# Block 1 of a quantized weight placed in two halves, and the first condition weights issued from another queue

## The reference

```python
W = weights[condition]                      # weights 16 x 64 x 64, condition 64
y = jnp.einsum('bct,bcd->bdt', x, W)        # x 64 x 64 x 1024, float32
v0 = p[:, :, 0] & 63; v1 = p[:, :, 0] >> 6 & 63; v2 = p[:, :, 1] & 63; v3 = p[:, :, 2] & 63
w = (unpacked.astype(jnp.float32) - zero_point) * scale      # 1024 x 1024, from qweight 1024 x 768 int32
out = x + jnp.einsum('bsk,nk->bsn', y, w) + bias
```

## Time and profile before

| | |
|---|---|
| median of the runs | 285.45 us |
| profiled execution | 285.6 us |
| its span, first to last instruction | 283.8 us |
| TensorE busy | 277.3 us, 98% of the span |
| VectorE busy | 191.8 us, 68% |
| ScalarE busy | 83.8 us, 30% |
| GpSimd busy | 99.2 us, 35% |
| granted TensorE clock, mean | 0.998 |

### The profile page before, as it was taken

The page is one execution under the profiler, slowest core; times in us unless marked ns, Lnnn a source line. Parts: engine busy times, 40 slices in busy tenths (PEclk is TensorE's granted clock), DMA queues, the critical chain, the costliest instruction groups (busy, mean ns, idle before and its releaser), DMA issues.

```text
span 283.8 us, 8491 instructions
## 1 busy us (share of the span) xinstructions
PE 277.3 (98%) x3307; PEld 231.4 (82%) x3307; DVE 191.8 (68%) x261; ACT 83.8 (30%) x169; POOL 99.2 (35%) x41
## 2 busy tenths in 40 slices
PE   7999999899999999999999999999999999999995
PEld 3888888788888888988888888888888888888885
DVE  2898897785566566865559555676667655595554
ACT  3795334241044300633017310443106330060000
POOL 4005903964430444314442444404443044430000
PEclk9999999999999999999999999999999999999999
DMA  7930563446215541355114551145413562101112
GB/s 277 372 120 11 179 223 133 155 162 223 75 74 157 168 174 67 112 160 198 74 74 124 165 211 74 74 155 157 155 69 113 161 209 90 74 37 74 74 74 75
DMA packets 20278, 37.96 MB, mean 134 GB/s; under 512 B 6814, under 2 KB 7070, under 8 KB 20266
## 3 DMA queue, kind: packets, MB, share of 16 engines
q1 hardware_dynamic: 19322, 35.43, 36.6%
q10 hardware_dynamic: 944, 2.38, 2.3%
HBM read 21.02 MB, written 16.78 MB: 133 GB/s over the span
## 4 chain that ended last, share of the span: by engine, by line
PE 95%; DMA 2%; issue 1%; ACT 1%; DVE 0%; SPq 0%
PE o_ps L296 71%; PE y_ps L296 12%; PE y_ps L265 10%; DMA w_sb<-in_L_cond_weights_dram 2%; PE o_ps L265 1%; PE o_ps L278 0%; DMA ids<-in_itok_B_dram 0%; PE o_ps L307 0%; ACT qT L446 0%; PE y_ps L278 0%; PE y_ps L307 0%; ACT y_hi L430 0%; SPq L163 0%; DVE o_sb L625 0%; DVE o_sb L627 0%
## 5 line engine op out<-in xcount | busy, mean ns | idle before, releaser
L296 PE MATMUL o_ps<-qT,y_hi 128*128 128x512 f32 (+1 forms) x448 | 171.5, 386 | 0.5 <-ACT qT L446 0.5
L296 PE MATMUL o_ps<-qT,y_lo 128*128 128x512 f32 (+1 forms) x448 | 171.2, 385 | 0.0
L647 POOL TENSOR_TENSOR resid<-x_sb,bias_bc 128x1024 f32<-128x1024 f32 x32 | 95.8, 3001 | 151.1 <-DVE o_sb L549 130.7
L296 PEld LDWEIGHTS o_ps<-qT,y_hi 128*128 128x128 f32 x448 | 83.6, 188 | 17.5 <-ACT qT L446 0.7
L296 PEld LDWEIGHTS o_ps<-qT,y_lo 128*128 128x128 f32 x448 | 83.6, 188 | 16.8
L541 DVE TENSOR_TENSOR o_sb<-o_ps,scale_bc 128x512 f32<-128x512 f32 x54 | 37.4, 692 | 73.5 <-PE o_ps L296 73.5
L430 ACT ACTIVATE y_hi<-y_ps 128x512 fp32r<-128x512 f32 x56 | 29.4, 610 | 96.7 <-PE y_ps L265 96.4
L549 DVE TENSOR_TENSOR o_sb<-o_sb,resid 128x512 f32<-128x512 f32 x63 | 51.5, 822 | 1.9
L421 ACT ACTIVATE junk<-x_sb 128x1024 bf16<-128x1024 f32 x32 | 33.9, 1058 | 63.3 <-DMA x_sb<-in_x_dram 63.3
L530 DVE SCALAR_TENSOR_TENSOR resid<-zs_bc,ysum,resid 128x1024 f32<-128x1024 f32 x32 | 44.8, 1403 | 0.0
L520 DVE TENSOR_TENSOR y_lo<-y_ps,y_hi 128x512 fp32r<-128x512 f32 x57 | 35.7, 689 | 5.4 <-ACT y_hi L430 5.4
(11 more groups left out here) (44 smaller groups left out, 71.1 us busy)
## 6 DMA issues: line engine op xcount, KB each, us to landing
x_sb<-in_x_dram SPq DMA_DIRECT2D x32, 512.0 KB, 3.4
out_dram<-o_sb SPq DMA_DIRECT2D x63, 256.0 KB, 2.1
q_raw<-in_L_ffn_qweight_dram ACTq DMA_DIRECT2D x6, 384.0 KB, 5.8
w_sb<-in_L_cond_weights_dram SPq DMA_DIRECT2D x63, 16.0 KB, 2.0
q_raw<-in_L_ffn_qweight_dram SPq DMA_DIRECT2D x2, 384.0 KB, 7.4
out_dram<-o_sb SPq DMA_DIRECT2D x2, 128.0 KB, 1.9
ids<-in_itok_B_dram SPq DMA_DIRECT2D x1, 0.2 KB
w_sb<-in_L_cond_weights_dram ACTq DMA_DIRECT2D x1, 16.0 KB, 3.6
```

Of the source, the lines that this page charges most:

```text
L296: last = nc.tensor.matmul(bank, part[:, slot, kt, :], qT[:, kt, col:col + width], start=(kt == 0 and part is y_hi), stop=(kt == KT - 1 and ...
L647: nc.gpsimd.tensor_tensor(resid[:, j % RING, :], x_sb[:, j % RING, :], bias_bc[:], ALU.add).then_inc(xbias_ready, 1)
```

## The change

Tile 0's condition weights are both issued from ScalarE's queue, each after its number is read. SyncE reads the two numbers of tile 1, issues tile 1 of x, and then both halves of tile 1's condition weights. Block 1 is placed by two instructions of 512 elements a row instead of one of 1024, with a semaphore after each, and the products of `y_hi` in `first_quarter` wait for the first half before their first four and for the second before their last four. VectorE no longer waits for ScalarE before it copies half 1 of `y_hi`; the wait, now for both halves, stands before `y_lo`.

```diff
             load_x(0, 0)
             sp.wait_ge(ids_loaded, 16)
-            load_w_half(sp, 0, 0, pick_first(sp, 0))
+            picked = [pick_first(sp, 2 + half) for half in range(2)]
             load_x(1, 0)
             for half in range(2):
-                load_w_half(sp, 1, half, pick_first(sp, 2 + half))
+                load_w_half(sp, 1, half, picked[half])
...
+            pe.wait_ge(qt_ready, 1)
+            pe.wait_ge(qt_half_ready, 1)
+            pe.wait_ge(y_hi_ready, 2)
+            first_quarter(y_hi, range(0, KT // 2))
             pe.wait_ge(qt_ready, 2)
-            pe.wait_ge(y_hi_ready, 2)
-            first_quarter(y_hi)
+            first_quarter(y_hi, range(KT // 2, KT))
...
+            def place_q_halves(n):
+                act.wait_ge(qt_ps_ready, n + 1)
+                for half, done in enumerate((qt_half_ready, qt_ready)):
+                    kts = slice(half * (KT // 2), (half + 1) * (KT // 2))
+                    nc.scalar.activation(qT[:, kts, n * P:(n + 1) * P], qt_banks[n % 2].bitcast(I16)[:, kts, :],
+                                         ACT.Copy, bias=-QCENTER).then_inc(done, 1)
...
-            load_w_half(act, 0, 1, pick_first(act, 1))
+            for half in range(2):
+                load_w_half(act, 0, half, pick_first(act, half))
             for n in (2, 3, 5, 7):
                 load_q(act, n)
             place_q(0)
             high(0, 0, y_banks[0], range(1))
-            place_q(1)
+            place_q_halves(1)
...
+                if whole:
+                    dve.wait_ge(y_hi_ready, t * 2 + 2)
                 for half in range(2):
-                    dve.wait_ge(y_hi_ready, t * 2 + half + 1)
+                    if not whole:
+                        dve.wait_ge(y_hi_ready, t * 2 + half + 1)
...
             dve.wait_ge(y_ps_ready, 2)
-            dve.wait_ge(y_hi_ready, 1)
             nc.vector.tensor_copy(y_hi[:, 0, :, S:2 * S], y_banks[0][1]).then_inc(y_hi_ready, 1)
-            low(0, 0, y_banks[0])
+            low(0, 0, y_banks[0], whole=True)
```

More of the change, by code:

```diff
@@ L122, in adaln_ffn @@
         qt_ready = sem("qt_ready")
+        qt_half_ready = sem("qt_half_ready")
         warm_ready = sem("warm_ready")
@@ L355, in left_half, with first_quarter @@
                 return products(o_ps[:, 0, :], 0, NH, 1, kts)
-            def first_quarter(part):
-                return products(o_ps[:, 0, 0:2 * P], 0, 2 * P, 0, parts=(part,))
+            def first_quarter(part, kts=range(KT)):
+                return products(o_ps[:, 0, 0:2 * P], 0, 2 * P, 0, kts, parts=(part,))
             pe.wait_ge(warm_ready, 1)
@@ L513, in spread, with low @@
                 nc.vector.stream_shuffle(row[:], row[:], mask=[0] * QUADRANT).then_inc(s, 1)
-            def low(j, i, banks):
+            def low(j, i, banks, whole=False):
                 t = i * RING + j
+                if whole:
+                    dve.wait_ge(y_hi_ready, t * 2 + 2)
                 for half in range(2):
-                    dve.wait_ge(y_hi_ready, t * 2 + half + 1)
+                    if not whole:
+                        dve.wait_ge(y_hi_ready, t * 2 + half + 1)
                     cols = slice(half * S, (half + 1) * S)
```

## The result

The changed kernel takes 288.23 us (median of 6 runs, 287.43 to 289.52) against 285.53 us (6 runs, 285.0 to 285.9): ratio 1.0089, 95% interval 1.0068 to 1.0111, so slower by 0.9% or about 2.5 us (the medians differ by 2.7). Forecast were 286.15 us and a range of 285.0 to 286.6. The direction was right, the size was not. The execution profiled first is the shortest of the six, 287.43 us with a span of 285.6.

The account below looks back on a forecast made before the run. TensorE was taken to bound the kernel without slack. The work edits' -0.34 us, with q2 landing 1.05 us later, came to +0.71: profiled 285.6 becomes 286.3, or 286.15 us against the median, range 285.0 to 286.6.

Parts of the forecast that it names:

- The bound and the carry: TensorE, busy 277.3 of 283.8 us: any shift at the start of tile 0's `y_lo` products (10.89 us) passes fully into the time.
- VectorE's wait and the two halves: Start-up, block 1: copy without its wait and placing in halves start the `y_lo` products near 10.55, not 10.89: -0.34 us.
- The order of transfers: DMA queues at start-up: tile 1 of x goes ahead of q2 and of tile 0's second weight half, making q2 late.
- q2 lands 1.05 us later: q2's DMA behind tile 1 of x: landing at 8.65 instead of 7.6, `y_lo` products at 11.60, +0.71 us in all.
- bounds of 0.95 and 1.28: q2's delay in us: 0.95 if moved side by side with tile 1 of x, 1.28 if wholly behind it.
- transfers of 128 rows proceed nearly in the order of issue: Trace reading of the start-up DMAs: large transfers go one after another, not side by side, at 0.41 MB/us.
- The condition weights: Rival, chance 0.12: tile 0's second weight half lands behind all of tile 1, at 8.15; mix at 8.29; +0.95, 286.4 us.
- its sign of 1.4 us: TensorE waiting over 1.4 us for tile 0's condition weights would show that the weights case holds.
- Of these nothing is waited for at its old time: SyncE's queue: tile 1 of x, its weights, q4 and q6 go out earlier, q4 and q6 about a microsecond; no cost counted.
- The clock: TensorE after the longer waits: a granted clock below 1.00 would add a cost, counted at nothing.
- Instruction fetch: Rival, chance 0.07: shifted code makes TensorE's 1.2 us wait near 49 us vanish or grow, 284.9 or 287.3 us.

Follow-up runs that it names:

- e1_compute: The changed kernel with the DMA queues of the kernel before, so only the work edits remain; 285.75 us, ratio 0.9999 to the kernel before.
- e7_cold: The changed kernel without the two warm-up matmuls ahead of tile 0's mix; 288.75 us, ratio 1.0101 to the kernel before.
- e11_x1_first: The kernel before with one line moved: SyncE issues tile 1 of x right behind tile 0, before waiting for the condition numbers; 287.74 us, ratio 1.0058.
- e4_x1_last: The changed kernel with both halves of tile 1's condition weights issued ahead of tile 1 of x on SyncE's queue; 288.81 us, ratio 1.0091 to the kernel before.
- the second profile: Profile of a repeat of the changed kernel, unaltered; the repeat measured 289.20 us, ratio 1.0118 to the kernel before.
- e3_q46_last: The changed kernel with q4 and q6 issued behind the three rows on SyncE's queue, after q3, q5 and q7; 288.00 us, ratio 1.0087 to the kernel before.
- e14_q2_first: The changed kernel with only one of three rows ahead of tile 1 of x, its weights behind, q4 and q6 last; 287.08 us, ratio 1.0050 to the kernel before.

## Why the prediction was right or wrong

**The bound and the carry: right from the sums on, wrong before them.** The loop adds nothing to a shift. But "whatever the change does to the start of tile 0's `y_lo` products is what it does to the time" doesn't hold. These products came 1.12 us later and the sums 1.58, with the wait for q3 between them. For a gain, too, "no slack in which a shift could vanish" was too strong: with the queues of before, VectorE's wait for q4 and the wait for instructions took back what `e1_compute` had gained.

**VectorE's wait and the two halves: right as work.** The copy follows the unpacking directly in every profile with VectorE's wait removed but `e7_cold`, where it waits 0.44 us for the slow mix. With q2 at its old time the `y_lo` products come 0.26 and 0.29 earlier (forecast 0.34). Worth in time: 0.9999, so nothing, where -0.34 had gone into the sum.

**The order of transfers: the right direction, and the step that failed.** Tile 1 of x moves first, the weights and q2 are late, and `e11_x1_first` shows that this order alone costs time. What failed is the term "q2 lands 1.05 us later" with its bounds of 0.95 and 1.28. Six profiles with the changed kernel's order of issue have q2 unpacked at 8.99, 9.61, 10.11, 10.44, 10.78 and 11.11, so 1.4 to 3.5 us late, all above the upper bound. The bounds rest on the reading that "transfers of 128 rows proceed nearly in the order of issue", so that only the bytes of tile 1 can come ahead of q2. Three other things go with its delay. With nothing of tile 1 ahead, q2 is still 0.6 to 0.7 late, which goes with its issue 1 us later. The small packets of tile 1's weights, ahead too, are worth 0.4 to 0.5. And what is issued behind q2 gets in as well: tile 1 of x in `e4_x1_last`, and q4 in the changed kernel, issued at 4.59, 0.44 behind q2. I had q4 move up "about a microsecond"; it moved up by 1.42. From 8 to 8.75 us of the first profile, with tile 1 of x landed and q2 not:
```profile
q1 hardware_dynamic: 77, 0.24, 85.2%
q10 hardware_dynamic: 22, 0.04, 12.8%
```
SyncE's packets here are of 3.1 KB on average, the row of a q block (3 KB) and not of x (4 KB): the later issued q4 moves, and ScalarE's queue nearly stands. From 8 to 10 us of the second profile both queues move at once, SyncE's more:
```profile
q1 hardware_dynamic: 135, 0.39, 56.7%
q10 hardware_dynamic: 91, 0.26, 35.1%
```
q2 was still on its way in that stretch, since it is unpacked at 10.78, and SyncE's packets, of 2.9 KB on average, are again rows of a q block. So q4 shares with ScalarE's loads, q2 among them. How much of q2's delay that is stays open: the one run that takes q4 away, `e3_q46_last`, has q2 at 9.34, within the scatter.

The rule of the Trainium skill (DMA: Bandwidth & Descriptors, Queues, rings and completion order), round-robin packet by packet, fits this last stretch roughly and not the one from 5.7 to 6.4 us, where one queue moved 68 packets and the other 12.

**The condition weights: a rival that was half right.** The second half landed behind all of tile 1, as its case said (mix at 8.54 against 8.29), and the wait passed its sign of 1.4 us (1.65). The forecast had the mix near 7.75, half of the way. The weights were not what bound: in the first profile `y_lo` ends at 10.62 + 1.29 = 11.91 on q2's path and is used at 12.01, and with the weights in time (`e4_x1_last`) the loss stays.

**"Of these nothing is waited for at its old time": wrong.** q4 and q6 moved up ahead of q3, and VectorE waits 0.52 us for q3; 0.49 us is lost behind q2 in the first profile. I had asked who waits for the moved transfers, not whom they pass.

**The clock, counted at nothing: wrong.** The prediction named the sign and gave it no price. Ten of twelve runs show a lower mean clock, and a fall costs 0.6 to 1.5 us.

**Instruction fetch: neither of my cases.** The wait near 49 us lies between 0.92 and 1.70 over all profiles, without a pattern with the code that I can name.

Added up for the execution profiled first, 287.43 against the 286.3 of the forecast: q2 0.34 later than in the sum (1.39 for 1.05), q3 about 0.5, the wait for instructions 0.2. The median, 288.23, is 0.8 above that execution, and the second profile shows what a longer run has: q2 later still, and the clock.

What stays open: why q2's landing scatters over two microseconds with the same order of issue, what lets one queue run ahead of the other, why `e14_q2_first` is 0.7 us slower in the median than in its profiled execution (286.36), and the clock's share of the median. The sizes don't split cleanly either. Tile 1 of x ahead, even earlier than in the change, costs 1.0058 (1.7 us). The change with tile 1 moved behind q2 costs 1.0050 (1.4 us), part of it for a later q4. The work edits cost nothing. The whole measures 2.5 to 3.4; that the first two add to 3.1 may be chance.

## What to carry to other kernels

When a transfer moves to another place or queue, list everything that it passes and everything that now lies behind it, in the order of issue over all queues; those whose consumer had no slack pay. Don't bound the delay by the bytes issued ahead: here transfers issued behind q2 got in as well, and q2 was 1.4 to 3.5 us late where those bytes gave 1.28. A moved issue isn't free because the engines are busy at the moment: q2, issued 1 us later, landed 0.6 to 0.7 later with nothing of the next tile ahead. Look at several executions before you put a number on a landing. And a gain at one point of a start-up like this is kept only if the next input is there too.

## What was not expected of the hardware

A 16 KB weight half issued at 2.60 us took 5.1 us to land while a 512 KB transfer, issued by the other queue at 2.8, took 5.2: from 5.7 to 6.4 us, 68 packets of the latter's queue moved against 12. Two loads issued 0.05 us apart in the same order were served one after the other in the kernel before and side by side in `e4_x1_last`, where the first of them landed 2 us later. One profile shows a clock of 1.00 while the same matmuls take 1.99 us instead of 1.16, because its clock records begin only at 13.75 us; durations are the safer reading. The wait for instructions at the first pass of the loop varies by up to 0.8 us between kernels whose loop is the same.
